# A mask tile of its own for the first query row of a self-attention group, and the first 512 mask columns made at the group's third step

## The reference, cut to what matters

```python
z = T * sigmoid(x.mean(axis=1) @ span_w + span_b)          # one span for each batch and head
dist = clip(idx[:, None] - idx[None, :], 0.0, None)
scores = einsum('bhtd,bhsd->bhts', q, k) / SCALE            # causal: keys after the query are NEG_INF
attn = softmax(scores, axis=-1)
mask = clip((R + z[:, :, None, None] - dist) / R, 0.0, 1.0) # R = 256
attn = attn * mask
attn = attn / (attn.sum(axis=-1, keepdims=True) + 1e-08)
out = einsum('bhts,bhsd->bhtd', attn, v)
```

## Time and profile before

| | |
|---|---|
| three runs | 3301.55, 3301.56 and 3304.24 us, median 3301.56 |
| profiled execution | span 3301.3 us |
| PE busy | 2990.0 us, 91% of the span |
| DVE busy | 1859.6 us, 56% |
| ACT busy | 1063.0 us, 32% |
| POOL busy | 943.3 us, 29% |
| the self-attention stage | about 327 to 1825 us of the span |

### The profile page before, as it was taken

One profiled execution on the slowest core, in us unless ns is written; L12 is line 12 of the kernel. 1 busy time (PEld: TensorE's weight loads), 2 busy tenths in 40 slices (PEclk: granted clock), 3 DMA queues, 4 the chain that ended last, 5 costly groups with the idle time before them and its releaser, 6 DMA issues. The chain is left out here.

```text
span 3301.3 us, 54795 instructions
## 1 busy us (share of the span) xinstructions
PE 2990.0 (91%) x19242; PEld 1673.0 (51%) x19242; DVE 1859.6 (56%) x2220; ACT 1063.0 (32%) x2510; POOL 943.3 (29%) x606
## 2 busy tenths in 40 slices
PE   8998799999999999999999789999999787777778
PEld 6876333333333333333333678888888343333335
DVE  4355878787887878787883345555554510000038
ACT  3222344444444444444444223333333100101123
POOL 0000554445444444445454022222222000000013
PEclk9999899999999999999999889999999888878889
DMA  4453512121212212131200411111111669999954
GB/s 166 178 204 128 128 49 62 51 70 44 70 53 55 69 48 60 52 73 43 69 16 4 150 42 64 64 64 64 64 64 65 243 249 420 420 421 420 421 226 162
DMA packets 181219, 438.54 MB, mean 133 GB/s; under 512 B 17470, under 2 KB 51928, under 8 KB 156457
## 3 DMA queue, kind: packets, MB, share of 16 engines
q1 hardware_dynamic: 174057, 425.19, 36.8%
q10 hardware_dynamic: 6976, 10.75, 0.9%
HBM read 351.74 MB, written 83.89 MB: 132 GB/s over the span
## 5 line engine op out<-in xcount | busy, mean ns | idle before, releaser
L785 ACT ACTIVATE B_e<-B_pS 128x512 f32<-128x512 f32 (+3 forms) x1280 | 619.2, 534 | 850.0 <-PE B_pS L865 427.9
L640 POOL TENSOR_TENSOR B_em<-B_e,B_mask 128x1024 f32<-128x1024 f32 (+1 forms) x320 | 670.9, 2098 | 730.7 <-ACT B_e L785 693.9
L703 DVE TENSOR_REDUCE mx<-B_pM 128x4 f32<-128x2048 f32 (+2 forms) x299 | 588.9, 1969 | 38.7 <-PE B_pM L847 20.3
L865 PE MATMUL B_pS<-B_qs,B_ks 128*128 128x512 f32 (+3 forms) x1280 | 505.2, 447 | 43.4 <-issue 19.7
L696 DVE SCALAR_TENSOR_TENSOR B_em<-B_mask,B_e 128x1024 f32<-128x1024 f32 (+1 forms) x320 | 354.4, 1108 | 257.9 <-PE B_pN L895 256.3
L865 PEld LDWEIGHTS B_pS<-B_qs,B_ks 128*128 128x128 f32 x1280 | 227.8, 192 | 363.1 <-issue 238.5
L883 PE MATMUL B_pD<-B_e,B_tiny 128*32 128x512 f32 (+3 forms) x2560 | 310.0, 557 | 0.0
L889 PE MATMUL B_pD<-B_em,B_ones 128*32 128x512 f32 (+3 forms) x2560 | 301.2, 543 | 0.3 <-DVE B_em L696 0.3
L895 PE MATMUL B_pN<-B_em,B_v 128*32 128x512 f32 (+3 forms) x2560 | 293.4, 530 | 0.0
L2089 PE MATMUL E_pI<-ring,hT 128*32 128x512 f32 x1024 | 184.5, 815 | 101.1 <-DMA ring<-in_L_ffn_e_W_dram 57.8
L2012 DVE TENSOR_TENSOR E_ug<-E_pT,bT 128x32 f32 x32 | 5.7, 192 | 445.2 <-PE E_pT L2099 445.2
(11 more groups left out here) (288 smaller groups left out, 4764.2 us busy)
## 6 DMA issues: line engine op xcount, KB each, us to landing
ring<-in_L_ffn_e_W_dram SPq DMA_DIRECT2D x128, 1024.0 KB, 21.8
ring<-in_L_ffn_e_Wg_dram SPq DMA_DIRECT2D x64, 1024.0 KB, 23.6
B_qs<-q_hi SPq DMA_DIRECT2D x64, 256.0 KB, 4.5
B_ks<-k_hi SPq DMA_DIRECT2D x64, 256.0 KB, 3.9
E_xq<-xT_sc ACTq DMA_DIRECT2D x18, 512.0 KB, 10.3
ring<-x_sc SPq DMA_DIRECT2D x36, 256.0 KB, 2.6
qc<-in_x_dram SPq DMA_DIRECT2D x34, 256.0 KB, 2.7
qc<-a_sc SPq DMA_DIRECT2D x34, 256.0 KB, 3.0
```

What stands on the lines that cost most here:

```text
L640: nc.gpsimd.tensor_tensor(em[:, f % SLOTS_EM, DVE_HEADS:, w0:], e[:, f % SLOTS_E, DVE_HEADS:, w0:], mask[:, DVE_HEADS:, u0:u0 + BLK - w0], ...
L703: nc.vector.tensor_reduce(mx[:, :, qt, c], pM[:, :, 0:w], AX.X, ALU.max).then_inc(max_taken, 1)
L785: nc.scalar.activation(e[:, f % SLOTS_E, h, w0:], pS[:, h % SBANKS, w0:], ACT.Exp, scale=SCALE).then_inc(exp_ready, 1)
L865: last = nc.tensor.matmul(pS[:, h % SBANKS, w0:], ks[:, kb // NT, h, kb % NT * P:(kb % NT + 1) * P], qs[:, qb, h, w0:], start=True, stop=( ...
```

## The change

A second, small tile `mask_row0` (128 x 4 x 512) holds the same numbers as chunk 0 and is read by query row 0's steps alone, all four diagonal. For the next group it is made at f = 24 to 27, one head a step, at steps at which `plan` makes nothing. Chunk 0 of `mask` itself, which is first read at step (1, 1), f = 5, is made at f = 2 of its own group, behind that step's `weigh` on DVE and ahead of its `reduce_unit`. The spans are taken at f = 24 instead of 28. The head 3 of chunk 1 goes back from f = 41 to f = 40, the step that the ramp of chunk 0 leaves. `RAMPS` counts the new semaphore steps.

```diff
+        mask_row0 = sb("B_mask_row0", [P, HPG, BLK], F32)
+        row0_ready = sem("B_row0_ready")
...
@@ both weigh functions (POOL's shown)
                 if kb == 0:
-                    pool.wait_ge(mask_ready[qb], it + f // STEPS + 1)
+                    pool.wait_ge(mask_ready[qb] if qb else row0_ready, it + f // STEPS + 1)
+                if (qb, kb) == (1, 1):
+                    pool.wait_ge(mask_ready[0], it + f // STEPS + 1)
+                weights = mask[:, DVE_HEADS:, u0:u0 + BLK - w0] if qb else mask_row0[:, DVE_HEADS:, u0:u0 + BLK - w0]
...
-            def ramp(it, c, heads, final):
+            def ramp(it, c, heads, final, row0=False):
 
                 t = slice(c * BLK, (c + 1) * BLK)
+                to, at, told = (mask_row0, slice(0, BLK), row0_ready) if row0 else (mask, t, mask_ready[c])
                 for h in heads:
-                    last = nc.vector.tensor_scalar(mask[:, h, t], ndist[:, t], span[:, h:h + 1], 0.0, ALU.add, ALU.max)
+                    last = nc.vector.tensor_scalar(to[:, h, at], ndist[:, t], span[:, h:h + 1], 0.0, ALU.add, ALU.max)
...
-            ramp(0, 0, range(HPG), True)
+            ramp(0, 0, range(HPG), True, row0=True)
...
-            RAMPS = 1 + (BPB - 1) * (HPG - DVE_HEADS)
+            RAMPS = 1 + BPB * (HPG - DVE_HEADS)
             ramps[0] = first_ramps
             plan = {28 + NT * (BPB - 1 - c) + h + 1: (c, h) for c in range(BPB - 1, 0, -1) for h in range(HPG)}
-            plan[STEPS + 1] = plan.pop(STEPS)
+            row0_plan = {24 + h: h for h in range(HPG)}
...
-                    if f == 28 and not final:
+                    if f == 24 and not final:
                         take_spans(it, (it + 1) * HPG, it + 2)
-                    if f == STEPS and not final:
-                        dve.wait_ge(masked_last, it * STEPS + STEPS)
-                        carry(dve, dve_carried)
-                        ramp(it, 0, range(HPG), True)
...
+                    if f == 2:
+                        dve.wait_ge(masked_last, it * STEPS + 2)
+                        carry(dve, dve_carried)
+                        ramp(it, 0, range(HPG), True)
                     if final and later:
                         continue
                     reduce_unit(it + later, n)
+                    if f in row0_plan:
+                        ramp(it, 0, [row0_plan[f]], row0_plan[f] == HPG - 1, row0=True)
```

More of the change, by code:

```diff
@@ L640, in weigh @@
                 nc.gpsimd.tensor_tensor(em[:, f % SLOTS_EM, DVE_HEADS:, w0:], e[:, f % SLOTS_E, DVE_HEADS:, w0:],
-                                        mask[:, DVE_HEADS:, u0:u0 + BLK - w0], ALU.mult).then_inc(masked_last, 1)
+                                        weights, ALU.mult).then_inc(masked_last, 1)
             def divide(it, qb):
@@ L679, in ramp @@
                     carry(dve, dve_carried)
-                    last = nc.vector.tensor_scalar_min(mask[:, cut[0]:cut[-1] + 1, t], mask[:, cut[0]:cut[-1] + 1, t], 1.0)
+                    last = nc.vector.tensor_scalar_min(to[:, cut[0]:cut[-1] + 1, at], to[:, cut[0]:cut[-1] + 1, at], 1.0)
                 if final:
-                    last.then_inc(mask_ready[c], 1)
+                    last.then_inc(told, 1)
             def take_spans(it, at, n):
@@ L692, in weigh @@
                 if kb == 0:
-                    dve.wait_ge(mask_ready[qb], it + f // STEPS + 1)
+                    dve.wait_ge(mask_ready[qb] if qb else row0_ready, it + f // STEPS + 1)
+                if (qb, kb) == (1, 1):
+                    dve.wait_ge(mask_ready[0], it + f // STEPS + 1)
+                weights = mask[:, 0:DVE_HEADS, u0:u0 + BLK - w0] if qb else mask_row0[:, 0:DVE_HEADS, u0:u0 + BLK - w0]
                 dve.wait_ge(exp_ready, it * HPG * STEPS + HPG * f + DVE_HEADS + SBANKS)
                 dve.wait_ge(mixed, it * STEPS + STEPS + f + 1 - SLOTS_EM)
-                nc.vector.scalar_tensor_tensor(em[:, f % SLOTS_EM, 0:DVE_HEADS, w0:], mask[:, 0:DVE_HEADS, u0:u0 + BLK - w0], 1.0,
+                nc.vector.scalar_tensor_tensor(em[:, f % SLOTS_EM, 0:DVE_HEADS, w0:], weights, 1.0,
                                                e[:, f % SLOTS_E, 0:DVE_HEADS, w0:], ALU.min, ALU.mult).then_inc(masked, 1)
@@ L770, in _ @@
                 group(it, False)
+            ramps[0] = first_ramps
             group(ITS - 1, True)
```

## The result

The changed kernel took 3311.93 us (median of six runs, 3309.91 to 3316.54), the kernel before beside it 3301.69 (3299.81 to 3304.24): a ratio of 1.0039 [1.0029, 1.0050] (in brackets the 95% interval, here and below), 10.2 us slower. The forecast was slower, by 27.7 us: the sign was right and the size 17.5 us too large. The profiled execution's span is 3309.4 us. All of the difference arises in the self-attention stage: the first matmul behind it starts at 1837.12 us in the trace of before and at 1846.80 in this one, 9.7 later; what follows is 1.6 us shorter in this trace.

A forecast was written before the change was run, and what follows sets the result against it. It took DVE's chain at each group boundary, up to unit 22, as the bound. Back edges 9.6, last boundary 4.4, first group 2.5 and clock 11.2 gave +27.7 us on 3301.3: 3329 us, 8 in 10 from 3296 to 3337.

The forecast's parts named there:

- The 2.7 us taken off the head of step 0: At each boundary, chunk 0's ramp (2.5 us) and the wait behind it (0.2) leave DVE's chain ahead of step 0.
- the 2.0 us forecast ahead of the inversions: Before DVE's inversions at a boundary, POOL's multiplications delay chunk 1's head 3: its ramp by 0.3, its minimum by 1.7 us.
- The last boundary: The seventh boundary, without a branch's slack: unit 22 at 1668.0, +4.4 us, and 1.6 more for the clock.
- the first group +2.5: The first group gets a ramp it did not have, ahead of unit 21's reduction: +2.5 us, nothing added for the clock.
- Row 0's mask: At f = 24 to 27 DVE's extra 0.5 us a step (1.0 with the minimum) was to cost nothing.
- DVE's branch: Rival: DVE's longer loop makes it wait at its branch, up to 3 us a back edge; 3347 at worst, likelier 3335; chance 0.06.
- So 1.6 us more at each of the seven boundaries: +11.2: Behind unit 22, PE's clock falls after a 4.3 us wait, so unit 23 follows in 4.79 us instead of 3.19.
- All three fall between 544.2 and the reduction ... so 3.0: At step 2, POOL's `divide` and its `weigh` of steps 2 and 3 delay DVE by 3.0 us ahead of unit 22.
- Back edges: Six boundaries with a branch: unit 22 goes at 552.6 instead of 551.03, +1.6 us each, +9.6 in sum, without the clock.
- everything from unit 22 on follows PE and repeats: From unit 22 to the group's last steps nothing else changes, so unit 22's lateness was taken as the group's.
- in the chain above: Moving head 3 from f = 41 to 40 was counted within DVE's boundary chain, with no term of its own.
- the "nothing to see" case: Rival: one POOL collision a boundary (1.3 us) of the four; back edges about 0, 3306 us in total; chance 0.15.

The follow-up runs named there:

- the second trace: The changed kernel as it is, run once more on a second chip: 3312.26 us, 1.0036 of the kernel before.
- either ACT run: Changed kernel with chunk 0's four ramps made by ACT, DVE keeping the minimum: 3285.00 us; the same with chunk 1's head 3 back at f = 41: 3280.88 us.
- the spread kernel: Changed kernel with chunk 0's ramp in three pieces behind the reductions: heads 0 and 1 at f = 2, head 2 at 3, head 3 at 4: 3305.67 us, 1.0021.

## Why the forecast had the sign and not the size

**Right.** The 2.7 us taken off the head of step 0 came: unit 19 to unit 20 is 3.61 us instead of 6.34. The ramp wasn't saved by it, and put a wait ahead of unit 22 at all seven boundaries, as said, though at three of the six back edges it is shorter than the 3 to 5 us named (2.3 to 2.7 in either trace) and at the last longer (7.3). One POOL multiplication gets in beside a ramp, a minimum or a `weigh`: of the 2.0 us forecast ahead of the inversions 1.4 are there (the minimum lost 1.82 - 0.43; the ramp ahead of it, 0.48, lost nothing of its 0.3), and the run with POOL's work cut short shows that without these turns the back edges would be faster than before. (The Trainium skill, SBUF — State Buffer, section "Who interferes with whom", says this of the DVE instructions that use the ports shared with GpSimd: one engine holds them for a whole instruction. The traces agree beside POOL's multiplications, with 1.10 us for a minimum of 16 elements, and not beside POOL's own ramps, where two of DVE's took 0.87; the measurement decides.) The last boundary was forecast at +4.4 + 1.6 = +6.0 and measured +5.6, the first group +2.5 and measured +3.0, and both are close in part by luck: at the last boundary the lateness of unit 22 was 3.1 and not 4.4 and the clock cost 2.5 and not 1.6; in the first group it was 2.2 with 0.8 for the clock, to which I had given nothing. Row 0's mask cost nothing (0.9999). DVE's branch didn't stall: what ended DVE's idle time ahead of 547.81 was PE's `mix`.

**Where it was wrong.** Three terms:

1. "So 1.6 us more at each of the seven boundaries: +11.2", the clock. It was paid at three of the six back edges (4.8 of 9.6; at four of six in the second trace) and at the last boundary, 2.5 for 1.6: 7.3 of 11.2, and 0.8 in the first group. I took the clock behind a wait of 4.6 us in the first group for the rule, and forecast a wait of 4.3; it was 2.59 at the odd boundaries, with the granted clock at 1.00 behind it, and 3.33 at the even ones, with 0.50. The second trace, with 1.00 behind 2.59 us and 0.50 behind 2.60, shows that the length of this wait alone doesn't give the number.
2. "All three fall between 544.2 and the reduction ... so 3.0", POOL's instructions beside step 2. Put back by the 3.24 us by which this group already ran late, unit 22 of the first boundary is at 554.51 - 3.24 = 551.27, not 552.6. Only the remainder of `divide` (0.3) and one `weigh` (1.0) fell there; POOL's `weigh` of step 3 came when DVE had gone on to the reduction, which it doesn't delay. At the even boundaries it was 1.0 + 1.0. Back edges were forecast at +1.6 without the clock, so 9.6 in sum; measured with the clock they are +5.6, and 5.6 - 3 x 1.6 = 0.8 without it.
3. Not forecast at all: the rests, -5.2. I took "everything from unit 22 on follows PE and repeats", and it doesn't: three of the seven rests of before have a 3.4 us stretch at half clock, and none of the changed kernel's has, in either of its traces. This gain was luck for the change: nothing in its edit aims at it. I had read one rest of seven.

In sum 27.7 - 4.8 (clock, three back edges for six) - 8.8 (turns) + 0.5 (first group) - 0.4 (last boundary) + 0.7 (the stage's start and end) - 5.2 (rests) is 9.7, which is the trace's.

**What I had under a wrong heading.** The move of head 3 from f = 41 to 40, which "is in the chain above", had 2.0 us of DVE's time in that chain, and there all of it went into the slack ahead of PE's `mix`: by my numbers it cost nothing at a back edge and 2.0 at the last boundary. The run without it says 10 to 12 us: 6 x (28.14 - 26.66) = 8.9 at the back edges and 29.79 - 28.50 = 1.3 at the last. Its 1.4 us of waiting for POOL don't reach PE through DVE's own queue but by shifting the inversions, and with them POOL's `divide`, onto `weigh` of step 2 and the ramps, and without that shift PE's wait ahead of unit 22 is 2.3 us at all six back edges, with the clock full behind it. The change without this line ends, in total, at the "nothing to see" case, though not by its parts.

**Open.** What decides that the clock falls in the middle of a group (three of seven rests before and with row 0's mask unread, in other groups; none in the changed kernel's two traces or in the one with head 3 at f = 41; one in either ACT run) isn't settled, nor is it behind unit 22, where 2.59 and 2.60 us of waiting had different ends in one trace. Nor is why the branch costs PE 2.9 to 4.2 us in different kernels, by which the even and the odd boundaries may differ. And the 22 us of the run with POOL cut short aren't split between the change's turns and those that the kernel before has too.

## What to carry to other kernels

When an edit ends a wait of one engine (POOL for the mask), list what this engine now runs and beside whose instructions: DVE stood still beside POOL's multiplications by whole instructions, and a minimum of 16 elements did so too, so five small ones belong where POOL waits, or on ACT, which took four of them off and gave 0.5%. An instruction that is hidden on its own engine can still set when another engine's next one falls; test a moved line by itself, since here one such line was worth ten microseconds. Add up the stage over all its repeats, not over one: nearly a third of the error (5.2 of 17.5 us) lay in stretches that the view of one group didn't show.

## What the runs showed of the hardware

- **DVE beside POOL's multiplications.** DVE's fp32 minimum of 128x512: 0.43 us alone, 1.80 to 1.86 beside one POOL multiplication; four ramps 1.67 alone, 2.69 with one POOL instruction in between, 4.13 with two; a minimum of 128x16 1.10. POOL's own multiplications of 768 columns took 1.80 to 2.23 there. DVE's reductions of 128x2048 from `pM`, in PSUM, did not grow: 187 of them ran beside a POOL multiplication after 420 us of the changed kernel's trace and took 2.23 to 2.30 us, the 15 others 2.28 to 2.29.
- **DVE beside POOL's `tensor_scalar`.** Two DVE ramps took 0.87 us inside one POOL ramp of 2.16, and a `weigh` of 1024 columns 2.07 instead of 1.23 beside POOL's minimum of 2.77, ending before it (the run in which POOL makes its own half).
- **The same work on three engines.** A ramp of 128x512 (two operations with one scalar per partition) took 0.48 us on DVE (1.67 for four), 2.07 on POOL, and 0.71 to 0.74 as a Relu with bias on ACT (2.57 for four).
- **The clock.** Behind a wait of 3.0 to 3.3 us ahead of unit 22 it was at half for 3.4 us each time in the changed kernel's two traces; behind 2.3 to 2.7 it stayed full but for one wait of 2.60, with which it was at half for 6.8, begun within the wait. In other places of the same stage it fell where PE had waited only 1.96 us (the spread kernel), or after a wait of 1.1 us (the three stretches in the middle of a group before), which stands in the other groups too, without a fall. I can give no rule for it.
